# First layer's keys held twice with zeros for the other head, and the scores as five whole-array products

## The chip, the cores and the metric

The kernel runs on one core of one Trainium2 chip. The metric is the device time of one execution in microseconds (us). TensorE (PE in the rows; PEld is its weight load) multiplies into PSUM, VectorE is DVE, ScalarE is ACT, GpSimd is POOL, SyncE is SP and issues most DMAs.

## What is computed

The reference is a small early-fusion model over 8 images with their texts. What matters here, cut to its core:

```python
edge = abs_scharr(gray(x)); text = bigram_embed(x_txt)     # 256 + 128 tokens of width 256 per image
# layer 0: attention with 16 heads of 16 columns, then two MLPs (gelu; ternary relu)
q = q * cos + _rotate_half(q) * sin
k = k * cos + _rotate_half(k) * sin
scores = jnp.einsum('bhqd,bhkd->bhqk', q, k) / math.sqrt(hd)
scores = jnp.where(causal[None, None], -jnp.inf, scores)
attn = jax.nn.softmax(scores, axis=-1)
attn_out = jnp.einsum('bhqk,bhkd->bhqd', attn, v)
# layer 1: grouped attention with 16 heads of 64 columns and ALiBi, then a mixture of 8 experts
```

A sequence has S = 384 tokens, in NT = 3 tiles of P = 128. The scores are causal: query tile t needs keys of tiles 0 to t, so 128, 256 and 384 columns.

## The kernel before

**Stages.** A prologue loads the inputs, makes the grey images, the text rows and the first image's queries and keys. Then come 16 units of attention, written out by hand as one order of calls per engine: eight of layer 0 (`U_FIRST`, five times `U_MID0`, `U_SIX`, `U_SEVEN`) and eight of layer 1. A unit of layer 0 does the attention of image u, and in its gaps the MLPs of image u-1 (`s2`), the queries and keys of image u+1 (`s1`) and the convolution of image u+2 (`conv`). `U_FIRST` has no MLPs, `U_SIX` no convolution and with it no residual additions on GpSimd (L3212, L3216), `U_SEVEN` makes no keys of layer 0. The expert stage follows the last unit.

**Precision in layer 0.** Each head's 16 columns are split into an upper part and a rest. `stack_upper_half` (ACT, L1677) and `stack_lower_half` (DVE, L2314) write four combinations, 64 rows per head, into `stk_q` and `stk_k`. `stack_turned` (PE, L1042) turns them with four 128-column products per tile into a PSUM bank, which holds 4 pairs of heads. ScalarE copies the queries to `q0T` (L1692), VectorE the keys to `k0T` (L2327). Both have 128 partitions: rows 0 to 63 are the first head of a pair, 64 to 127 the second. The copies of a unit are named (hh, t): hh is the half of the heads, t the tile of tokens. Three copies of hh = 0 must be done before the unit's `scores_ahead`, or in the prologue before the first scores.

**Banks.** PSUM banks 0 to 2 hold the scores of a pair, 3 and 4 the turned probabilities, 5 the outputs. All dense products of the units (projections, MLPs, stacks) take banks 6 and 7 in turn: the planner `dense_units` lists them in PE's order, the k-th has bank 6 + k % 2. `wait_free` makes PE wait until the engine that copies a bank out has increased `freed`. A copy out that takes longer holds up PE's next use of that bank.

**Scores.** `pair_scores` (L950) gives the scores of heads 2p and 2p+1 with six products: stationary are 128 columns of the queries of one head (64 rows), moving are the keys of the same head. The order alternates the halves of the array. (s, 1) of both heads share bank 2; the semaphore `first_half` makes PE wait before it writes bank 2 for the second time. `filled[1]` is given after the fourth product, `filled[2]` after the fifth, `filled[0]` after the sixth. On VectorE `mask_max_of` (L2270) waits for `filled[s]` and `filled[2]`, adds the mask and finds the row maxima; ScalarE makes the exponentials, PE turns them (L978), ScalarE and VectorE copy them to `probsT` (L1733, L2429), and PE multiplies them with the values (L1013).

**Neighbours of the copies on VectorE's list in a unit of layer 0:** (0,0), take_turned(7), mask_max(10); mask_max(11), (0,1), take_turned(8), weigh(0); mask_max(12), (0,2), mask_max(13), stack_lower(1); mask_max(15), (1,0), hidden(0), hidden(1); take_turned(14), (1,1), mask_ahead(1); take_turned(15), (1,2), invert_last of the next unit.

**GpSimd in the prologue:** it clears `gray` (L3120) and `vpad` (L3121, 1536 elements a partition), then waits for the text index; later it gathers text rows and experts' rows with indirect DMAs. VectorE waits for `cleared` before the grey image (L2810).

Of the kernel before, what the change touches and what calls it, by code (L numbers as in the profile page):

```python
# [20 lines left out]
F32 = mybir.dt.float32  # L21
F32R = mybir.dt.float32r
# [5 lines left out]
P = 128  # L28
B = 8
# [4 lines left out]
S = IMG + TXT  # L34
NT = S // P
# [265 lines left out]
PAIRS = HEADS // 2  # L301
# [8 lines left out]
def at(u, per, k):  # L310


    reg, off = u
    return off * per + k if reg is None else reg * per + (off * per + k)


def moved(u, d):
    return u[0], u[1] + d
# [5 lines left out]
def early_fusion_kernel(nc, a, const, out):  # L324
# [10 lines left out]
    def sb(name, shape, dt=F32):  # L335
        at = offsets["top"]
        offsets["top"] = at + (width(shape) + 31) // 32 * 32
        return place(name, shape, dt, at)
# [9 lines left out]
    with ctx:  # L348
# [98 lines left out]
        rinvT = sb("rinvT", [P, S])  # L447
        qk_start = offsets["top"]
        q0T = sb("q0T", [P, 8, S], F32R)
        k0T = sb("k0T", [P, 8, S], F32R)  # L450
        (alibi,), _ = region(qk_start, ("alibi", [P, H1, S], F32))


# [59 lines left out]
        ps = [ctx.enter_context(nc.psum_tensor(f"bank{k}", [P, 512], F32)) for k in range(8)]  # L513


        filled = [sem(f"bank{k}_filled") for k in range(8)]
# [5 lines left out]
        cleared = sem("cleared")  # L522
# [42 lines left out]
        first_half = sem("first_half")  # L565
# [42 lines left out]
        def scores_place(n, t):  # L608

            if t == 1:  # L610
                return ps[2][:, 2 * P * (n % 2):2 * P * (n % 2) + 2 * P]
            return ps[n % 2][:, (3 * P, 0, 0)[t]:(4 * P, 0, 3 * P)[t]]
# [289 lines left out]
        def _(pe):  # L902
            mm, tr = nc.tensor.matmul, nc.tensor.transpose
# [46 lines left out]
            def pair_scores(layer, p, u):  # L950

                half = [slice(64 * s, 64 * s + 64) for s in range(2)]
                for b in range(3):
                    pe.wait_ge(freed[b], at(u, PAIRS, take0[b] + p))
                for s, t in ((0, 1), (1, 2), (0, 2), (1, 0), (1, 1), (0, 0)):
                    if layer == 0:
                        q, k = q0T[half[s], p, :], k0T[half[s], p, :]
                    else:
                        q, k = q1T[half[s], p, :], k1T[half[s], p // 4, :]
                    if (s, t) == (1, 1):  # L960
                        pe.wait_ge(first_half, at(u, PAIRS, p + 1))
                    last = mm(scores_place(s, t), q[:, P * t:P * (t + 1)], k[:, 0:P * (t + 1)], start=True, stop=True)  # L962
                    if (s, t) == (0, 1):
                        last.then_inc(first_half, 1)
                    if (s, t) == (1, 0):
                        last.then_inc(filled[1], 1)
                    if (s, t) == (1, 1):
                        last.then_inc(filled[2], 1)
                last.then_inc(filled[0], 1)
# [471 lines left out]
            for c in range(DC):  # L1441
                last = tr(ps[1][0:EMB, P * c:P * (c + 1)], proj_raw[:, c, :], ident)
# [5 lines left out]
            k = banks.bank(SETUP, "txt_index")  # L1448
# [3 lines left out]
            k = banks.bank(SETUP, "gamma")  # L1452
# [87 lines left out]
            bank = banks.bank(ROUTE, "thresholds")  # L1540
# [3 lines left out]
            for name, left in (("totals", "ones"), ("earlier", "before")):  # L1544
                bank = banks.bank(ROUTE, name)
                banks.wait_free(pe, ROUTE, name)
                mm(ps[bank][:, 0:2 * E * TILES], const_cols(left), sel_eq[:].rearrange("p k n -> p (k n)"),
                   start=True, stop=True).then_inc(filled[bank], 1)
# [3 lines left out]
            bank = banks.bank(ROUTE, "first_index")  # L1552
            banks.wait_free(pe, ROUTE, "first_index")
            for n in range(TILES):
                if n % 8 == 0:
                    pe.wait_ge(first_hot, n // 8 + 1)
                last = mm(ps[bank][0:CP, 0:CT], first_row[:, n, :], first_col[:, n, :],
                          start=(n == 0), stop=(n == TILES - 1))
# [492 lines left out]
        def _(dve):  # L2051
            v = nc.vector
# [193 lines left out]
            def first_norm_of(img_no, t):  # L2246
                normalise(LN_FIRST, img_no, mv_a, rstd_a, x1, h_in, t)
                then()
                moments(LN_ATTN0, stats_a, mv_a, x1, t)
# [76 lines left out]

            def take_stack_of(sec, i, hh, t):  # L2327
                k, f_ = bank_of(sec, f"stk{hh}_{t}_k", i)
                v.tensor_copy(k0T[:, 4 * hh:4 * hh + 4, P * t:P * (t + 1)],
                              k[:].rearrange("p (q n) -> p q n", q=4)).then_inc(f_, 1)  # L2330

            def values_of(sec, i, layer, t):
                k, f_ = bank_of(sec, f"v{layer}_{t}", i)
# [484 lines left out]
            k, f_ = bank_of(SETUP, "txt_index")  # L2818
# [27 lines left out]
            stack_lower_half(one, 0)  # L2846
            first_norm_of(two, 0)
            first_norm_of(two, 1)
            for t in range(NT):
                take_stack_of(PRO, 0, 0, t)  # L2850
            stack_lower_half(one, 1)
# [47 lines left out]
            k, f_ = bank_of(ROUTE, "by_group")  # L2899
            v.tensor_copy(by_group[:, 0:P], k[:, 0:P])  # L2900
            for h in range(2):
                rows, spot = slice(P // 2 * h, P // 2 * (h + 1)), slice(P + P // 2 * h, P + P // 2 * (h + 1))
                last = v.tensor_copy(by_group[rows, P:3 * P // 2], k[rows, spot])
# [3 lines left out]
            for r in range(SEARCH):  # L2907
                for q in range(STEPS):
                    last = ts(at_least[:, q, :], by_group[:], as_gate[:, q:q + 1], 0.0, ALU.is_ge, ALU.add,  # L2909
                              accum_out=cnt[:, q:q + 1])  # L2910
# [28 lines left out]
            k, f_ = bank_of(ROUTE, "thresholds")  # L2939
# [9 lines left out]
            k, f_ = bank_of(ROUTE, "totals")  # L2949
# [7 lines left out]
            k, f_ = bank_of(ROUTE, "earlier")  # L2957
# [50 lines left out]
            k, f_ = bank_of(ROUTE, "first_index")  # L3008
# [106 lines left out]
        def _(pool):  # L3115
            g = nc.gpsimd
# [2 lines left out]
                g.nop().then_inc(freed[bank], 1)  # L3119
            g.memset(gray[:], 0.0)  # L3120
            g.memset(vpad[:], 0.0).then_inc(cleared, 1)  # L3121

            banks.wait_taken(pool, SETUP, "txt_index")
            def gather_text(b):
# [260 lines left out]
```

## Time and profile before

| what | value |
|---|---|
| median of three runs | 1880.91 us (1877.96 to 1881.28) |
| the profiled execution | 1881.84 us, its span 1880.0 us |
| TensorE, matmul busy | 1751.2 us (93%) in 11231 |
| TensorE, weight load busy | 1427.0 us (76%) |
| VectorE busy | 1248.4 us (66%) in 4073 |
| ScalarE busy | 967.2 us (51%) |
| GpSimd busy | 545.7 us (29%) |
| mean granted clock of TensorE | 0.969 |
| indirect DMAs of GpSimd | 8 for the text, 3 x 64 for the experts |

Busy times of TensorE are modelled at their ends and overlap one another; two neighbouring starts say more than a duration. In a timeline a row that stands for several instructions has the start of the first and the time to the end of the last. Idle time in square brackets is that before the row, with what ended it.

### The profile page before, as it was taken

Reading aid. Unit: us, or ns where it says so; the run is one execution under the profiler, and the core shown is the slowest. Engines: PE = TensorE matmul, PEld = TensorE weight load, DVE = VectorE, ACT = ScalarE, POOL = GpSimd, SP = SyncE. Lnnn points to the kernel's source line nnn. Section 1 sums busy time; section 2 is a strip of 40 time slices with the busy share of each in tenths; the row PEclk is TensorE's granted clock in tenths of the full one; section 3 lists DMA queues with packets and bytes.
Section 4 is the critical chain, followed back from the end, with each engine's and each line's share of the span. In section 5 each row is a group of like instructions: output and inputs, shape, how many; then the busy total and the mean of one; then the engine's idle time right before and its main releaser. Section 6 shows DMA issues by size and latency. Waiting matters only on the chain.

```text
span 1880.0 us, 33649 instructions
## 1 busy us (share of the span) xinstructions
PE 1751.2 (93%) x11231; PEld 1427.0 (76%) x11231; DVE 1248.4 (66%) x4073; ACT 967.2 (51%) x2669; POOL 545.7 (29%) x763
## 2 busy tenths in 40 slices
PE   5788999999999999899999999993999999999997
PEld 3455677776867677688888888872898999899896
DVE  5678787777778775857767777667744555454542
ACT  1355657575756766656667666640234334333421
POOL 2352433424242410111111111010434434533431
PEclk9698999999999999999999999995999999999998
DMA  6111020101001010103001110012232321122210
GB/s 212 41 37 66 1 63 10 54 10 54 29 18 60 1 35 1 35 5 92 23 13 35 35 35 27 1 45 68 88 102 68 107 91 54 46 81 67 65 41 22
DMA packets 74244, 91.03 MB, mean 48 GB/s; under 512 B 16524, under 2 KB 64311, under 8 KB 74073
## 3 DMA queue, kind: packets, MB, share of 16 engines
q1 hardware_dynamic: 61464, 67.90, 11.1%
q0 software_dynamic: 9472, 16.77, 3.2%
q10 hardware_dynamic: 3136, 4.21, 0.6%
q8 instruction: 91, 1.49, 0.3%
q14 instruction: 81, 0.66, 0.1%
HBM read 71.02 MB, written 25.00 MB: 51 GB/s over the span
## 4 chain that ended last, share of the span: by engine, by line
PE 75%; issue 9%; DVE 7%; POOL 3%; ACT 2%; DVEq 2%; POOLq 1%; DMA 1%; SPq 0%; ACTq 0%
PE bank L1601 17%; PE bank L1030 16%; PE bank L1616 10%; PE bank L978 7%; PE bank L962 6%; PE bank L1013 6%; PE bank L1190 3%; PE bank L934 2%; PE bank L1052 2%; PE bank L989 1%; PE bank L914 1%; PE bank L935 1%; DVE at_least L2909 1%; POOL rstd_b L3136 1%; PE bank L1582 1%
## 5 line engine op out<-in xcount | busy, mean ns | idle before, releaser
L1725 ACT ACTIVATE probs<-probs,nmax 128x128 f32<-128x128 f32 (+2 forms) x768 | 381.5, 501 | 55.7 <-DVE nmax L2286 55.4
L978 PE MATMUL bank<-cst,probs 128*128 128x128 f32 x1536 | 235.1, 278 | 14.5 <-ACT probsT L1733 11.3
L978 PEld LDWEIGHTS bank<-cst,probs 128*128 128x128 f32 x1536 | 179.8, 142 | 48.1 <-issue 20.1
L3178 POOL COPY rinv<-rowsum 128x384 f32<-128x384 f32 x80 | 40.9, 511 | 563.6 <-DVE rowsum L2302 321.4
L1601 PE MATMUL bank<-xeT,gate_w 128*128 128x480 f32 x768 | 187.5, 379 | 0.5 <-issue 0.5
L1601 PE MATMUL bank<-xeT,up_w 128*128 128x480 f32 x768 | 186.8, 378 | 0.0
L3072 DVE TENSOR_TENSOR prod<-bank,sil 128x480 f32<-128x480 f32 x128 | 84.0, 657 | 147.6 <-PE bank L1601 146.8
L1616 PE MATMUL bank<-down_w,hT 128*120 128x256 f32 x1536 | 181.3, 280 | 0.0
L1616 PEld LDWEIGHTS bank<-down_w,hT 128*120 128x120 f32 x1536 | 179.9, 181 | 0.1
L1733 ACT COPY probsT<-bank 128x384 f32<-128x384 f32 x256 | 121.6, 475 | 107.4 <-PE bank L978 71.9
L1646 ACT ACTIVATE sil<-bank 128x480 f32<-128x480 f32 x128 | 73.0, 570 | 175.8 <-PE bank L1601 175.7
L2429 DVE COPY probsT<-bank 128x384 f32<-128x384 f32 x256 | 141.5, 553 | 30.3 <-PE bank L978 28.6
L1601 PEld LDWEIGHTS bank<-xeT,up_w 128*128 128x128 f32 x768 | 144.8, 189 | 21.6 <-DVE up_w L3004 0.2
L1601 PEld LDWEIGHTS bank<-xeT,gate_w 128*128 128x128 f32 x768 | 144.2, 189 | 21.5 <-issue 0.6
L1725 ACT ACTIVATION_READ_ACCUMULATOR probs<-probs,nmax 128x1 f32 x768 | 146.6, 191 | 0.0
L2286 DVE CUSTOM_DVE_ANT_0 probs<-bank,alibi 128x128 f32<-128x128 f32 (+2 forms) x384 | 141.7, 420 | 2.0 <-issue 0.3
L3354 POOL DMA_INDIRECT out<-ye,slot_token x64 | 75.5, 1180 | 229.7 <-DVE ye L3085 217.8
L2286 DVE CUSTOM_DVE_ANT_0 probs<-bank,cst 128x128 f32<-128x128 f32 (+2 forms) x384 | 140.9, 419 | 0.0
L962 PE MATMUL bank<-k1T,q1T 64*128 64x256 f32 (+2 forms) x768 | 100.5, 394 | 2.9 <-DVE nmax L2286 2.9
L3324 POOL DMA_INDIRECT xe<-xn_rows,slot_token x64 | 70.9, 1108 | 93.0 <-DVEq L3010 52.4
L962 PEld LDWEIGHTS bank<-k1T,q1T 64*128 64x128 f32 x768 | 83.3, 186 | 18.4 <-issue 12.9
L1013 PE MATMUL bank<-probsT,v 128*64 128x384 f32 (+2 forms) x768 | 97.0, 388 | 0.0
(350 smaller groups left out, 3422.3 us busy)
## 6 DMA issues: line engine op xcount, KB each, us to landing
gate_raw<-in_L_ffn_gate_w SPq DMA_DIRECT2D x8, 1024.0 KB, 4.8
up_raw<-in_L_ffn_up_w SPq DMA_DIRECT2D x8, 1024.0 KB, 6.9
down_raw<-in_L_ffn_down_w SPq DMA_DIRECT2D x8, 1024.0 KB, 5.7
img<-in_x SPq DMA_DIRECT2D x8, 768.0 KB, 5.1
residual_rows<-x SPq DMA_DIRECT2D x8, 384.0 KB, 2.5
residual_rows<-h_in SPq DMA_DIRECT2D x8, 384.0 KB, 3.6
xr<-residual_rows SPq DMA_DIRECT2D x8, 384.0 KB, 4.7
hr<-residual_rows SPq DMA_DIRECT2D x8, 384.0 KB, 3.6
```

The costliest lines, as they stand in the source:

```text
L962: last = mm(scores_place(s, t), q[:, P * t:P * (t + 1)], k[:, 0:P * (t + 1)], start=True, stop=True)
L978: last = tr(ps[bank][:, P * q:P * (q + 1)], probs[:, n % 4, SEG[t] + P * j:SEG[t] + P * (j + 1)], ident)
L1013: last = mm(ps[5][rows_o, P * j:S], w, probsT[:, n % 4, cols_j], start=first, stop=final)
L1030: last = mm(ps[bank][:, 0:width], x, w, start=(k == 0), stop=(k == len(pieces) - 1))
L1601: last = mm(ps[bank][:, 0:HALF], w[:, wp, c, P * m:P * (m + 1)], xeT[:, xp, c, HALF * hf:HALF * (hf + 1)], start=(c == 0 and k == 0), stop ...
L1616: last = mm(ps[bank][:, D * (j % 2):D * (j % 2) + D][0:CP], hT[:, j // 4, hp, m, CP * (j % 4):CP * (j % 4 + 1)], down_w[:, wp, m, :], star ...
L1725: last = f(p, p, ACT.Exp, bias=nmax[:, n % 4, t:t + 1], scale=-1.0, accum_out=rowsum[:, where, t:t + 1])
L1733: nc.scalar.copy(probsT[:, n % 4, 0:3 * P], ps[3][:, 0:3 * P]).then_inc(freed[3], 1)
L2286: last = v.tensor_tensor_reduce(out=probs[:, n % 4, seg(t)], in0=scores_place(n, t), in1=bias[:, P * (2 - t):S], scale=1.0, scalar=BIG, op ...
L2429: v.tensor_copy(probsT[:, n % 4, 3 * P:6 * P], ps[4][:, 0:3 * P]).then_inc(freed[4], 1)
L3072: tt(prod[:, q % 2, :], k[:, 0:HALF], sil[:, q % 2, :], ALU.mult).then_inc(f_, 1)
L3354: g.indirect_dma_start(out_rows, slots(e, j), ye[0:CP, j, :], None, bounds_check=T - 1, oob_is_err=False).then_inc(scattered, 16)
```

## The change

`k0T` gets a further dimension of two: for each head of the pair a whole 128-row key array, in which the 64 rows of the other head are zero. GpSimd clears all of it once, 128 partitions of 8 x 2 x 384 = 6144 elements. VectorE's copy of a key stack becomes two, each of 64 partitions, into the place of its head; the bank is given free behind the second. `pair_scores` in layer 0 multiplies all 128 rows of the queries (both heads) with such a key array; the zeros take the other head out. The middle tile does both heads at once, with 2 x 256 moving columns into all of bank 2. The order is: 512 columns, then per head 384 and 128; `filled[2]` comes after the first product, `filled[0]` after the third and `filled[1]` after the fifth. `first_half` is no more used in layer 0. SBUF for k0T grows by 12 KiB a partition; the scratch of GpSimd's descriptors is set to 4096 bytes.

```diff
-        k0T = sb("k0T", [P, 8, S], F32R)
+        k0T = sb("k0T", [P, 8, 2, S], F32R)
...
                 for b in range(3):
                     pe.wait_ge(freed[b], at(u, PAIRS, take0[b] + p))
+                if layer == 0:
+                    queries = [q0T[:, p, P * t:P * (t + 1)] for t in range(NT)]
+                    mm(ps[2][:], queries[1], k0T[:, p, :, 0:2 * P], start=True, stop=True).then_inc(filled[2], 1)
+                    for s, bank in ((0, 0), (1, 1)):
+                        mm(scores_place(s, 2), queries[2], k0T[:, p, s, :], start=True, stop=True)
+                        mm(scores_place(s, 0), queries[0], k0T[:, p, s, 0:P], start=True, stop=True).then_inc(filled[bank], 1)
+                    return
                 for s, t in ((0, 1), (1, 2), (0, 2), (1, 0), (1, 1), (0, 0)):
-                    if layer == 0:
-                        q, k = q0T[half[s], p, :], k0T[half[s], p, :]
-                    else:
-                        q, k = q1T[half[s], p, :], k1T[half[s], p // 4, :]
+                    q, k = q1T[half[s], p, :], k1T[half[s], p // 4, :]
                     if (s, t) == (1, 1):
-                        pe.wait_ge(first_half, at(u, PAIRS, p + 1))
+                        pe.wait_ge(first_half, at(moved(u, -B), PAIRS, p + 1))
...
                 k, f_ = bank_of(sec, f"stk{hh}_{t}_k", i)
-                v.tensor_copy(k0T[:, 4 * hh:4 * hh + 4, P * t:P * (t + 1)],
-                              k[:].rearrange("p (q n) -> p q n", q=4)).then_inc(f_, 1)
+                for s in range(2):
+                    rows_s = slice(64 * s, 64 * s + 64)
+                    last = v.tensor_copy(k0T[rows_s, 4 * hh:4 * hh + 4, s, P * t:P * (t + 1)],
+                                         k[rows_s, :].rearrange("p (q n) -> p q n", q=4))
+                last.then_inc(f_, 1)
...
             first_norm_of(two, 1)
+            dve.wait_ge(cleared, 2)
             for t in range(NT):
                 take_stack_of(PRO, 0, 0, t)
...
             g.memset(vpad[:], 0.0).then_inc(cleared, 1)
+            g.memset(k0T[:].bitcast(F32), 0.0).then_inc(cleared, 1)
...
-    nc = bacc.Bacc("TRN2", target_bir_lowering=False, num_devices=1)
+    nc = bacc.Bacc("TRN2", target_bir_lowering=False, num_devices=1, dynamic_dma_scratch_size=4096)
```

## Rows read from the trace of the kernel before

**Rows 1.** Busy time by stretch: span, PE, PEld, DVE, ACT, POOL, granted clock, DMA

```profile
359.20:445.30 86.10, 84.03 (x541) 63.05 (x541) 67.26 (x226) 54.98 (x160) 31.13 (x52) 1.00 0.11 35
...
137.00:157.00 20.00, 11.24 (x89) 8.56 (x89) 18.30 (x74) 14.91 (x52) 2.61 (x7) 0.80 0.00 1
```

**Rows 2.** Waits of PE in one steady unit: total us, times, longest

```profile
PE bank L1030 <- ACT relu L1646: 0.9, 1, 0.9
```

**Rows 3.** Timeline of PE: start us, us, what, count

```profile
421.72 0.66 PE L1052 MATMUL bank<-ident_r,stk_k 128*128 128x128 f32 x4
422.22 0.51 PE L978 MATMUL bank<-cst,probs 128*128 128x128 f32 x3
422.49 4.08 PE L1190 MATMUL bank<-f2T,hid_parts 128*128 128x256 f32 x32
426.40 0.56 PE L1052 MATMUL bank<-ident_r,stk_q 128*128 128x128 f32 x4
...
427.08 0.66 PE L1052 MATMUL bank<-ident_r,stk_k 128*128 128x128 f32 x4
427.67 0.82 PE L962 MATMUL bank<-k0T,q0T 64*128 64x256 f32 x6
428.43 0.53 PE L1013 MATMUL bank<-probsT,vpad 128*32 128x384 f32 x4
...
1500.37 1.44 PE L1601 MATMUL bank<-xeT,up_w 128*128 128x480 f32 x6
1501.65 1.44 PE L1601 MATMUL bank<-xeT,gate_w 128*128 128x480 f32 x6
```

**Rows 4.** The key copy, by its line: ns min/median/max, first and last start

```profile
L2329 DVE CAST k0T<-bank x48: 657/685/692, 80.0 to 679.7; 128x512 fp32r<-128x512 f32 x48
```

**Rows 5.** Groups of DVE by line and shape: busy us, mean ns

```profile
L2108 DVE TENSOR_TENSOR hashf<-hashf 8x128 f32<-8x128 f32 x1 | 0.3, 280 | 0.1
...
L2341 DVE TENSOR_TENSOR vpad<-bank,rows 128x128 f32<-128x128 f32 x6 | 1.4, 277 | 0.3 <-PE bank L1030 0.3
```

**Rows 6.** Timeline around copy (0,1) of a steady unit

```profile
392.66 0.69 DVE L2329 CAST k0T<-bank 128x512 fp32r<-128x512 f32 x1
...
393.28 0.56 DVE L2429 COPY probsT<-bank 128x384 f32<-128x384 f32 x1
...
393.57 0.61 PE L1052 MATMUL bank<-ident_r,stk_k 128*128 128x128 f32 x4
```

**Rows 7.** Timeline around copy (0,0)

```profile
385.79 0.69 DVE L2329 CAST k0T<-bank 128x512 fp32r<-128x512 f32 x1 [1.86 <-PE bank L1052]
...
386.66 0.86 PE L1030 MATMUL bank<-w,hidT 128*128 128x256 f32 x3
```

**Rows 8.** Timeline around copies (1,0) and (1,1)

```profile
410.53 0.69 DVE L2329 CAST k0T<-bank 128x512 fp32r<-128x512 f32 x1 [0.28 <-PE bank L1052]
...
411.35 0.94 PE L1030 MATMUL bank<-x_parts,f1T 128*128 128x384 f32 x4
...
411.58 2.15 POOL L3216 TENSOR_TENSOR h_in<-h_in,rows 128x768 f32<-128x768 f32 x1
...
411.96 1.99 DVE L2547 CAST hid_parts<-relu 128x384 fp32r<-128x384 f32 x1
...
423.09 0.68 DVE L2329 CAST k0T<-bank 128x512 fp32r<-128x512 f32 x1
```

**Rows 9.** Timeline of the prologue's key copies

```profile
81.86 0.69 DVE L2329 CAST k0T<-bank 128x512 fp32r<-128x512 f32 x1 [1.21 <-PE bank L1052]
...
92.31 1.11 PE L1052 MATMUL bank<-ident_r,stk_k 128*128 128x128 f32 x4 [1.51 <-DVE k0T L2329]
```

**Rows 10.** Start of the kernel: timeline of POOL and DVE, and L2065 by its line

```profile
1.84 1.38 POOL L3121 MEMSET vpad<- 128x1536 f32 x1
...
6.36 0.43 DVE L2232 TENSOR_SCALAR gray<-img 128x512 f32<-128x512 f32 x1 [2.40 <-DMA img<-in_x]
...
L2065 DVE TENSOR_SCALAR by<-tok x4: 272/277/766, 2.6 to 3.7; 8x258 int32<-8x258 int32 x4
```

## The prediction

> **What bounds the kernel now.** I read the page first (its figures are in the table above): TensorE is busy for 93% of the span, more than any other engine, though a busy TensorE is not one at its peak. Then I cut the first layer's stretch into its periods. One image's unit takes 86.1 us, and TensorE is busy for 84.0 of them at the full granted clock, VectorE for 67.3 [rows 1]. The waits of such a unit say the same: TensorE's longest is 0.9 us, on a ReLU of ScalarE [rows 2]. So in the steady units TensorE sets the time, and work given to VectorE is free only where nothing of TensorE waits for it. In the prologue and the first unit it is otherwise: between 137 and 157 us VectorE is busy for 18.3 of 20 us and TensorE for 11.2 [rows 1]; VectorE's own chain sets the pace there. Last I read the timelines around the touched lines, to see which wait stands right behind each.
>
> My sum is made against the profiled execution, 1881.84 us with a span of 1880.0; it lies 0.9 us above the median of the three runs, 1880.91.
>
> **Removed and put in its place: the products.** There were 384 half-array products (8 images, 8 pairs, 6 each). One set of six lasts 0.76 us from its first start to the next instruction's, from 427.67 to 428.43 [rows 3]. Going into it costs too: four 128-column products that are followed by a set take 0.59 us, the same four followed by transposes 0.50 [rows 3], so 0.09. Together 0.85 us. The five new ones are whole-array products of the same fast type with 512, 384, 128, 384 and 128 columns. From rows of that type: 32 products of 256 columns take 3.91 us, 0.122 each, and six of 480 take 1.28, 0.213 each [rows 3]. That is 0.41 ns a column, so 0.227 for 512 and 0.173 for 384; 128 columns take 0.11 to 0.125 (0.50 for four) [rows 3]. Sum 0.227 + 2 x 0.173 + 2 x 0.11 = 0.79 us. Bounds: from below the bare columns, 1536 at 2.4 GHz, 0.64 us; from above the four 128-column products' 0.125 for each short one and as much again between unequal widths, 0.95. I take 0.79, the nearest rows. So six of a unit's eight sets gain 0.06. The other two have a narrow neighbour (the 3-row products before scores(3), the 32-column products behind scores(1)) and keep that cost, so they lose 0.03 to 0.04. A unit gains 0.3 us, or 0.2 if the short products are at 0.125; I take 0.2 in each of seven units, **-1.4 us** (bounds -12 and +7).
>
> The set's row bears on a rule of the Trainium skill: 0.76 us for 1536 columns is more than the bare columns at the full clock, so the halves bought little. "TensorEngine Tiling (Array Packing)", sections Key Properties and Theoretical Speedup, says that products in different halves of the array run in parallel, up to twice as fast. By that rule the old set would need half its columns' time, 0.32 us, and the change would add 0.47 to each of 64 sets, 30 us; the measured 0.76 decides against it. No run here shows whether another order of the halves would come nearer.
>
> **Added: a second copy per key stack.** Each of 48 copies (PSUM to k0T, 128x512, 0.685 us [rows 4]) becomes two of 64 partitions, and the bank is freed behind the second. VectorE's duration does not follow the partitions: a 128-element tensor op takes 280 ns on 8 partitions and 277 on 128 [rows 5]. So each half costs what the whole did. One behind another, such copies start 0.61 apart (392.66 copy, 393.28 next op [rows 6]); I take +0.60 us. From below, 0.30 would be half the copy at half the partitions, and 0 if the two overlapped wholly; from above 0.69. 48 x 0.60 is 29 us of VectorE. What of it lies on TensorE's path:
>
> (0,0) of a steady unit: the copy ends at 386.48 and the next product into the same bank starts at 386.66 [rows 7]; TensorE's weight load waits for that bank. With 0.60 more the bank comes free at 387.08, TensorE starts near 387.19: +0.53. (0,1): copy from 392.66 to 393.35, the next stack product into that bank at 393.57 [rows 6]: free at 393.95, start at 394.06: +0.49. (1,0): the copy ends at 411.22, the product starts at 411.35 [rows 8]: +0.55, but here something takes it back. TensorE later waits 0.9 us for a ReLU [rows 2] that waits for hid_parts; the cast before it takes 1.99 us because a GpSimd op runs until 413.73 [rows 8]. A cast that starts 0.6 later ends with that op all the same, and the later wait shrinks by what the earlier one grew. I take 0 (bound +0.55). (0,2), (1,1), (1,2): the next user of the bank comes 0.6 us later or more. The tightest is (1,1): its copy ends at 423.77 [rows 8], the bank's next product is the seventeenth of those that start at 422.49 [rows 3], so 424.45. I take 0 (bound 0.1 together). Behind each copy VectorE's queue holds a probsT copy or a mask_max, which TensorE and ScalarE need; VectorE's idle spots (19 us a unit) absorb those. So 1.02 a unit, five units: **+5.1 us**. The sixth unit has no residual additions on GpSimd (no convolution), so (1,0) counts as well: **+1.6**.
>
> Prologue: the six stack products of a half alternate two banks. The copy of 81.86 ends at 82.55 and would end at 83.15; the next key product, 0.05 us behind it, moves along. At 92.31 such a product starts after TensorE has sat idle for 1.51 us on the copy before it [rows 9]. Each copy but (0,2) hands its +0.60 on: 5 x 0.60, **+3.0 us**. First unit: copies (0,0), (0,1), (0,2) lie in VectorE's closed stretch, +1.8; (1,0) half hidden, +0.3; (1,1) before mask_ahead, for which scores(1) waits, +0.6: **+2.7 us**.
>
> **Added: a memset of 6144 elements a partition on GpSimd.** vpad's 1536 take 1.38 us [rows 10], so four times as many 5.2 to 5.5 us, from 3.2 to about 8.5 us. GpSimd's own next work is at 34 us, and VectorE's wait for `cleared` comes at about 80 us: both hidden. But VectorE isn't: an op that ran beside the vpad memset took 766 ns against 277 for its like [rows 10]. The grey-image ops start at 6.36 [rows 10], at the head of the chain that ends last (grey image, halo transfer, convolution). The next token op, at 3.28, would stand until 8.5 and push the grey image to about 9: +2.6; if the token ops slip through first, +1.8. I take **+2.2** (bounds 0 and 2.8; a gain is excluded, as it only adds work).
>
> **Moved and dropped waits.** The wait on `first_half` goes with the old sets, priced within them; the second layer's keeps its meaning with counts shifted by one layer. Head 0's scores are ready after three products of five, some 0.25 us sooner; VectorE's mask_max is not what steady TensorE waits for, so 0. The descriptor scratch for GpSimd's indirect transfers shrinks; nothing in the trace shows it in use: 0, with a rival below.
>
> Sum: -1.4 + 5.1 + 1.6 + 3.0 + 2.7 + 2.2 = **+13.2 us**, 1894.1 against the median (1895.0 against the profile).
>
> **Rivals.** A change of 0.2% (3.8 us) is about what a measurement of this kernel can tell from none.
> (1) The bank waits stay but the new set runs at its columns' pace, 0.64: 48 sets x 0.21 and 16 x 0.11 save 12 instead of 1.4: +2.6 to +4 us, about 1884 to 1885, at the edge of no change. For: TensorE is the bound. Against: no row of that type is under 0.12 us for 256 columns.
> (2) The half copies cost half each, so nothing is added: -1.4 + 2.2 = +0.8, 1881.7, no change. Against: the 8-partition row.
> (3) Faster: the new set saves more than the copies cost. Place: the sets in the steady units, at 0.64 us (-12). It decides by over 3.8 us only if a copy adds under (12 - 3.8 - 2.2) / 20.7 = 0.29 us (my copy terms are 20.7 times 0.60). With copies at 0.15 it gives 12.4 / 4 - 12 + 2.2 = -6.7, 1874.
> (4) More stalls: (1,0) isn't absorbed in the five middle units (+2.8), or the longer idle of the first unit keeps TensorE's clock low for longer (the granted clock was 0.80 of full speed there on average [rows 1]): +3 to +6, 1897 to 1900.
> (5) The smaller scratch makes GpSimd wait in the expert stage, where indirect transfers follow one another: some us on each of eight experts, beyond 1900.
>
> **How the numbers follow.** Forecast 0.60; rival (1) 0.13, (2) 0.08, (3) 0.05, (4) 0.11, (5) 0.03. Slower: 0.60 + 0.11 + 0.03 + 0.10 of (1) = 0.84; same: 0.08 + 0.03 = 0.11; faster 0.05. The range reaches from rival (1) to rival (4), 1884 to 1900; it leaves out (2), (3) and (5), 0.16 in all.
>
> **What would show it.** Products: 320 in place of 384 on the new lines, a set at 0.79 us start to start. Copies: 96 of 64x512 at 0.69 us. Waits: TensorE on k0T near (0,0) and (0,1) of each unit, 0.5 us each; a unit's period 86.1 grown to 86.9. The grey image ending at 10 to 11 in place of 8.3 us. The start of the steady part 7 to 8 us later. I am wrong if the unit's period doesn't grow, or if a half copy takes under 0.5 us.

## The result, and the profile after

The changed kernel takes 1890.22 us (median of six runs, 1887.33 to 1891.88) where the kernel before, run beside it, takes 1881.10: ratio 1.0049, 95% interval 1.0037 to 1.0061, so +9.2 us (+7.0 to +11.5). Timed a second time it gave 1.0059 (1.0043 to 1.0075). It is slower, as forecast, and the time lies in the range; 1894.1 was 4 us too much. That closeness is in part luck, errors of opposite sign, as the runs show: the copies cost 6 to 9 us more than the forecast had, a gain of 5.6 us at the very end of the program stood in it at 0, and the products saved 2.7 us more.

| what | before | after |
|---|---|---|
| the profiled execution's span | 1880.0 us | 1886.4 us |
| TensorE, matmul busy | 1751.2 us in 11231 | 1750.0 us in 11167 |
| TensorE, weight load busy | 1427.0 us | 1444.2 us |
| VectorE busy | 1248.4 us in 4073 | 1283.2 us in 4121 |
| mean granted clock | 0.969 | 0.966 |
| a middle unit of layer 0 | 86.1 us | 87.25 us |
| GpSimd's last instruction, a DRAIN (from the trace's records) | 7.90 us | 2.34 us |

The middle unit that answers to [rows 1], cut at the same instruction (columns as there):

```profile
366.68:453.93 87.25, 84.53 (x533) 65.47 (x533) 70.09 (x232) 55.29 (x160) 30.85 (x52) 1.00 0.11 34
```

The unit is 1.15 us longer at the same full clock. TensorE is busy for 0.5 us more with 8 products fewer, VectorE for 2.8 us more with six copies more. TensorE's waits in it, beside [rows 2]:

```profile
PE bank L1034 <- DVE k0T L2335: 0.9, 2, 0.5
PE bank L914 <- DVE xh_b L2212: 0.7, 1, 0.7
PE bank L1056 <- DVE k0T L2335: 0.4, 1, 0.4
PE bank L982 <- ACT probsT L1737: 0.3, 1, 0.3
PE bank L1034 <- ACT relu L1650: 0.2, 1, 0.2
```

Three new waits for the copies of the key stacks, 1.3 us together, and the wait for the ReLU fallen from 0.9 to 0.2. The forecast had two of the three stalls, and the absorption of the third. The places, in time order, TensorE's rows and VectorE's copies:

```profile
394.57 0.45 PE L1034 MATMUL bank<-w,hidT 128*128 128x256 f32 x1 [0.50 <-DVE k0T L2335]
...
402.04 0.55 PE L1056 MATMUL bank<-ident_r,stk_k 128*128 128x128 f32 x3 [0.37 <-DVE k0T L2335]
...
420.37 0.98 PE L1034 MATMUL bank<-x_parts,f1T 128*128 128x384 f32 x4 [0.40 <-DVE k0T L2335]
...
422.88 1.87 PE L1034 MATMUL bank<-x_parts,f1T 128*128 128x384 f32 x8 [0.16 <-ACT relu L1650]
```

```profile
393.03 1.39 DVE L2335 CAST k0T<-bank 64x512 fp32r<-64x512 f32 x2 [1.72 <-PE bank L1056]
...
400.60 1.39 DVE L2335 CAST k0T<-bank 64x512 fp32r<-64x512 f32 x2
...
418.93 1.39 DVE L2335 CAST k0T<-bank 64x512 fp32r<-64x512 f32 x2 [0.29 <-PE bank L1056]
```

A pair of half copies takes 1.39 us where the whole one took 0.69 [rows 4]. Over all 96:

```profile
L2335 DVE CAST k0T<-bank x96: 650/689/695, 77.3 to 693.4; 64x512 fp32r<-64x512 f32 x96
```

(shortest, median and longest ns): 64 partitions cost what 128 did. The operation behind the copy starts 0.60 to 0.67 us after a whole copy's start, and 1.41 to 1.45 after a pair's, so VectorE's order moves back by 0.8 us each time. The set of products that answers to the one at 427.67 [rows 3]:

```profile
436.11 0.45 PE L957 MATMUL bank<-k0T,q0T 128*128 128x512 f32 x1
436.40 0.34 PE L959 MATMUL bank<-k0T,q0T 128*128 128x384 f32 x1
436.57 0.23 PE L960 MATMUL bank<-k0T,q0T 128*128 128x128 f32 x1
436.63 0.39 PE L959 MATMUL bank<-k0T,q0T 128*128 128x384 f32 x1
436.87 0.22 PE L960 MATMUL bank<-k0T,q0T 128*128 128x128 f32 x1
437.02 0.53 PE L1017 MATMUL bank<-probsT,vpad 128*32 128x384 f32 x4
```

From its first start to the next instruction's it lasts 0.91 us, not 0.79; the old one lasted 0.76. The unit's eight new sets last 0.75, 0.90, 0.84, 0.86, 0.84, 1.05, 0.84 and 0.84 us (means of four middle units), the old ones 0.75 or 0.76 each. What they gain lies ahead of them (the run of the products alone, below).

The start of the program, VectorE and then GpSimd:

```profile
2.68 6.44 DVE L2069 TENSOR_SCALAR by<-tok 8x258 int32<-8x258 int32 x4 [1.23 <-DMA tok<-in_x_txt]
9.05 0.41 DVE L2236 TENSOR_SCALAR gray<-img 128x512 f32<-128x512 f32 x1
```

```profile
3.15 5.22 POOL L3130 MEMSET k0T<- 128x6144 f32 x1
```

Four token operations that take 1.3 us without the memset last 6.44, and the grey image begins at 9.05 in place of 6.36 [rows 10].

The end of the program: the last indirect store of the kernel before is issued at 1869.11 and the span ends at 1880.0, 10.9 us later; after the change,

```profile
1880.95 1.01 POOL L3363 DMA_INDIRECT out<-ye,slot_token  x1 [0.30 <-issue]
```

and the span ends at 1886.4, 5.4 us later. From 1384 us on all of TensorE's starts and this store are 11.8 us later than before, the end of the span only 6.4. Between the two lies GpSimd's last DRAIN, 7.90 us long before and 2.34 after; it begins 2.8 us behind the last store's start in both.

**Two profiled executions carry different pieces of low clock**, so a difference of starts is read stretch by stretch. From the start of one unit's scores to the next one's, the five stretches of middle units and the sixth run at full clock, and repeat from execution to execution of one kernel to 0.1 us, the sixth to 0.3. The first 165 us and the end of layer 0 do not repeat. Nor does the stretch from 1260 to 1384 us: over it the changed kernel's profile gains 1.9 us on that of before, by shorter pieces of low clock. The profile has no record of the clock before its first piece of full clock (49.9 us in the kernel before) and counts that time as full, though products there run at the pace of the low clock; so its mean granted clock is a little too high.

### The profile page after: what moved, and what is told of

It reads as the page before. It is cut to its first block, busy times and chain, and to the rows that moved or that the text cites. A ratio compares the mean times of both kernels' runs of the same rounds, so it can differ in the third digit from the quotient of the medians.

```text
span 1886.4 us, 33571 instructions
## 1 busy us (share of the span) xinstructions
PE 1750.0 (93%) x11167; PEld 1444.2 (77%) x11167; DVE 1283.2 (68%) x4121; ACT 969.8 (51%) x2669; POOL 549.3 (29%) x764
## 3 DMA queue, kind: packets, MB, share of 16 engines
q1 hardware_dynamic: 61464, 67.90, 11.1%
## 4 chain that ended last, share of the span: by engine, by line
PE 75%; issue 9%; DVE 8%; POOL 2%; DVEq 2%; ACT 2%; POOLq 1%; DMA 0%; SPq 0%; ACTq 0%
PE bank L1605 17%; PE bank L1034 16%; PE bank L1620 10%; PE bank L982 7%; PE bank L1017 6%; PE bank L966 5%; PE bank L1194 3%; PE bank L934 2%; PE bank L993 1%; PE bank L1056 1%; PE bank L914 1%; DVE k0T L2335 1%; PE bank L959 1%; PE bank L935 1%; DVE at_least L2917 1%
## 5 line engine op out<-in xcount | busy, mean ns | idle before, releaser
L3333 POOL DMA_INDIRECT xe<-xn_rows,slot_token x64 | 71.6, 1118 | 89.6 <-DVEq L3018 51.8
```

## The experiments

Each was timed in five rounds beside the kernel before. The ratio is the one on record, with its 95% interval; it is not the quotient of the two medians (for e2_copies that would be 22.5 us and not 21). A difference in us below is the ratio's unless medians are named. "Middle unit" is the distance of two units' starts at full clock, from the trace.

| kernel | median us | before, beside it | ratio (95%) | middle unit | last DRAIN |
|---|---|---|---|---|---|
| e1_scratch | 1875.68 | 1879.38 | 0.9976 (0.9964 to 0.9988) | 86.06 | 2.34 |
| e2_copies | 1901.92 | 1879.38 | 1.0112 (1.0095 to 1.0130) | 87.78 | 7.90 |
| e3_products | 1875.89 | 1879.38 | 0.9978 (0.9966 to 0.9990) | 85.62 | 7.90 |
| e4_memset | 1878.92 | 1879.38 | 0.9998 (0.9987 to 1.0008) | 86.07 | 2.34 |
| e5_clear_act | 1892.22 | 1879.80 | 1.0061 (1.0048 to 1.0074) | 87.27 | 2.34 |
| e6_two_engines | 1884.74 | 1879.80 | 1.0023 (1.0013 to 1.0032) | 86.73 | 2.34 |
| e7_scratch2k | 1874.03 | 1879.80 | 0.9963 (0.9952 to 0.9975) | 86.06 | 0.71 |
| e8_behind | 1880.86 | 1879.80 | 1.0002 (0.9992 to 1.0013) | 86.53 | 2.34 |
| e9_change_again | 1892.65 | 1880.29 | 1.0059 (1.0043 to 1.0075) | 87.25 | 2.34 |
| e10_clear_again | 1890.30 | 1880.29 | 1.0049 (1.0035 to 1.0063) | 87.28 | 2.34 |

### The scratch alone

```diff
-    nc = bacc.Bacc("TRN2", target_bir_lowering=False, num_devices=1)
+    nc = bacc.Bacc("TRN2", target_bir_lowering=False, num_devices=1, dynamic_dma_scratch_size=4096)
```

> The kernel before with the descriptor scratch of 4096 bytes and nothing else. Theory A: the scratch sets how long GpSimd's last instruction, a DRAIN behind the last indirect store, takes (7.90 us before, 2.34 us after the change), so the time falls by 5.5 us, a ratio near 0.997, and all starts up to the last indirect store stay within 0.5 us apart from pieces of low clock. Rival B, my forecast: 0 us, the drain stays at 7.9 us (its length then hangs on what the queue still has to do). Rival C: waits of GpSimd in the expert stage, over +5 us.

The DRAIN took 2.34 us and the time fell by 4.5 us (2.3 to 6.8). The distance from the last store to the end of the span:

```profile
span 1877.8 us, 33649 instructions
```

```profile
1872.40 1.01 POOL L3354 DMA_INDIRECT out<-ye,slot_token  x1 [0.31 <-issue]
```

so 5.4 us, as after the change, in place of 10.9. Theory A holds: the last instruction's length follows the size of the scratch, the work in the queue being the same. Whether more or less work would change it too, no run tells. The expert stage was not longer: from 1384 us on, all starts of TensorE in the changed kernel stand 11.84 to 11.86 us behind those of before, to the last expert's end; in this run 3.28 to 3.30.

### A still smaller scratch

```diff
+    nc = bacc.Bacc("TRN2", target_bir_lowering=False, num_devices=1, dynamic_dma_scratch_size=2048)
```

> The kernel before with a descriptor scratch of 2048 bytes. Theory A: GpSimd's last DRAIN grows with the scratch's size (16384 bytes 7.90 us if that is the size before, 4096 bytes 2.34 us, a slope of 0.45 ns a byte), so it takes 1.4 us here and the time is 6.5 us under the kernel before. Rival B: the drain stays near 2.3 us. Rival C: the smaller scratch makes indirect transfers wait for room in the expert stage, an expert's 61 us grow, and the time is above that of the kernel before.

The DRAIN took 0.71 us, shorter than the straight line's 1.4 (from 4096 to 2048 bytes it lost 0.80 ns a byte; the expectation's 0.45 above that takes the size before as 16384, which no run prints), and the time fell by 7.0 us (4.7 to 9.0). The expert stage did not grow: from 1384 us on all starts of TensorE stand 0.43 us ahead of those of before. This kernel has the lowest median of all that were run, and of the change it has only the last line, with another size.

```profile
span 1872.7 us, 33649 instructions
```

```profile
1868.97 1.01 POOL L3354 DMA_INDIRECT out<-ye,slot_token  x1 [0.30 <-issue]
```

### The copies alone

```diff
-                v.tensor_copy(k0T[:, 4 * hh:4 * hh + 4, P * t:P * (t + 1)],
-                              k[:].rearrange("p (q n) -> p q n", q=4)).then_inc(f_, 1)
+                for s in range(2):
+                    rows_s = slice(64 * s, 64 * s + 64)
+                    last = v.tensor_copy(k0T[rows_s, 4 * hh:4 * hh + 4, P * t:P * (t + 1)],
+                                         k[rows_s, :].rearrange("p (q n) -> p q n", q=4))
+                last.then_inc(f_, 1)
```

> The kernel before with each copy of a key stack cut into two of 64 partitions, the old six products, no zeros, the old scratch. Theory A: the copies alone make the longer first layer: a middle unit +1.0 to +1.2 us, the prologue +3.0, the first unit +2.7 to +3.7, the sixth +1.6 to +2.2, in all +12.4 to +14.5 us, 1893.5 to 1895.5. Rival B: a part of the growth of a unit comes from the new products, so that a middle unit grows by 0.6 us or less here and the time by under 9 us. The GpSimd drain at the end stays at 7.9 us if the scratch sets it.

The time rose by 21 us (17.9 to 24.4), more than the whole change costs, and a middle unit by 1.71:

```profile
371.94:459.72 87.78, 85.06 (x541) 63.28 (x541) 71.15 (x232) 55.30 (x160) 30.77 (x52) 1.00 0.11 34
```

The copies alone make the loss; theory A holds for its place and was low for its size (1.0 to 1.2 us a unit and 12.4 to 14.5 in all expected). The starts of TensorE's products in this unit against those of before show where: +0.66 at the product behind copy (0,0), +0.56 behind (0,1), +0.68 behind (1,0) and +0.43 at a ReLU's bank soon after, of which 0.91 comes back at 415.25 (time of before), +0.16 at the MLP's second product behind (1,1), and +0.25 less 0.11 near 433. Sum 1.72. The last of these stands at a product (`wo,o0T`) for which the waits name no key copy; that it comes from VectorE's lateness behind (1,2), and not from a bank, is likely and not shown. From unit to unit the stretches of this run are longer than those of before by 3.6 us (prologue), about 3.1 (first unit, with the clock in it), 2.45, four times 1.71 and 2.3: 18 of the 21 us. The rest lies within the interval and was not traced.

### The products alone

```diff
+                if layer == 0:
+                    twice = k0T[:, p, 0:2 * P].unsqueeze(1).broadcast_to([P, 2, 2 * P])
+                    mm(ps[2][:], queries[1], twice, start=True, stop=True).then_inc(filled[2], 1)
+                    for s, bank in ((0, 0), (1, 1)):
+                        mm(scores_place(s, 2), queries[2], k0T[:, p, :], start=True, stop=True)
+                        mm(scores_place(s, 0), queries[0], k0T[:, p, 0:P], start=True, stop=True).then_inc(filled[bank], 1)
+                    return
```

> The five whole-array products in place of the six half-array ones, with the old key array and one copy per stack; left out are the zeros, so each head's scores are the sum of both heads' scores. Theory A: a set at 0.79 us where it was 0.76 plus 0.09 at its entry, -1.4 us in all (-0.2 a middle unit). Rival B: the set runs at its columns' pace, 0.64 us, and a middle unit is 1.5 us shorter, -12 us in all. Rival C: the new set costs 0.95 us, a middle unit +0.8, +7 us in all.

The time fell by 4.1 us (1.9 to 6.4), a middle unit by 0.45:

```profile
356.31:441.93 85.62, 83.45 (x534) 65.31 (x533) 66.09 (x226) 54.96 (x160) 31.11 (x52) 1.00 0.11 35
```

None of the three had it: the sign is A's, the size between A and B. The set that gains most, scores(5) behind `xTb,w`, in the kernel before and here:

```profile
377.65 1.78 PE L1030 MATMUL bank<-xTb,w 128*128 128x384 f32 x5
379.36 0.82 PE L962 MATMUL bank<-k0T,q0T 64*128 64x256 f32 x6
380.11 0.59 PE L1030 MATMUL bank<-xTb,w 128*128 128x384 f32 x1
```

```profile
376.24 0.69 PE L958 MATMUL bank<-k0T,q0T 128*128 128x512 f32 x1
...
377.28 0.54 PE L1035 MATMUL bank<-xTb,w 128*128 128x384 f32 x1
```

The old set lasts 0.75 us, the new one 1.04, and yet TensorE comes out of it 0.15 us ahead, because it goes in 0.45 sooner relative to the work ahead. The sets that gain nothing are the two with a narrow neighbour. Scores(3), behind the products of 3 rows, in the kernel before and here:

```profile
447.12 0.69 PE L935 MATMUL bank<-halo_gray,edge_w 3*128 3x256 f32 x2
447.74 0.83 PE L962 MATMUL bank<-k0T,q0T 64*128 64x256 f32 x6
448.50 1.55 PE L1030 MATMUL bank<-wqkv,xTa 128*128 128x512 f32 x3
```

```profile
444.04 0.69 PE L935 MATMUL bank<-halo_gray,edge_w 3*128 3x256 f32 x2
444.67 0.50 PE L958 MATMUL bank<-k0T,q0T 128*128 128x512 f32 x1
...
445.52 1.07 PE L1035 MATMUL bank<-wqkv,xTa 128*128 128x512 f32 x2
```

From the first row to the last it was 1.38 us and is 1.48. Now take each set from the start of the last product ahead of it to the start of the first behind it (means of four middle units). The eight sets, scores(0) to scores(7), took 1.02, 0.96, 0.95, 1.06, 0.95, 1.17, 0.95 and 0.96 us, and take 0.93, 1.01, 0.86, 1.16, 0.87, 1.07, 0.86 and 0.86: six gain 0.08 to 0.10, scores(1) and scores(3) lose 0.05 and 0.10, together 0.40 of the unit's 0.45. In six of the eight sets the product ahead starts 0.03 to 0.17 us before the new set, where it was 0.20 to 0.42; ahead of scores(1) 0.11 for 0.21, and ahead of scores(3) 0.30 in both. So the cost of the half-array set lay ahead of its first start more than in it, and the four-against-four comparison of [rows 3] (0.09) had only a part of it.

### Copies whole, and further work of VectorE behind them

```diff
                 v.tensor_copy(k0T[:, 4 * hh:4 * hh + 4, P * t:P * (t + 1)],
                               k[:].rearrange("p (q n) -> p q n", q=4)).then_inc(f_, 1)
+                v.tensor_copy(spare[0:64, t], cst[0:64, 0:704])
```

> The kernel before with the small scratch; each copy of a key stack is whole and frees the bank as before, and behind it VectorE makes a further copy of like length from constants in SBUF (64 x 704, about 0.7 us) that nobody reads. Theory A: the bank's hold makes the stalls, not VectorE's time: a middle unit grows by 0 to 0.5 us in place of 1.7, and the time, with the scratch's -5, is between -5 and +3 us. Rival B: VectorE's lost time makes them: a middle unit grows by 1.2 us or more, the time by +10 us or more.

The added copy took 0.51 us, not 0.7, but for (1,0), where it ran beside a GpSimd operation and took 0.87. A middle unit grew by 0.46 in place of 1.71, the time by 0.4 us (-1.5 to +2.4), with the small scratch in it. No bank is held longer, but VectorE's added work is not as much as in e2_copies: 2.3 us a unit against 3.9 (69.5 and 71.2 us busy, 67.3 before). The next operation starts some 0.4 us later than before at five of the six places, where e2_copies has 0.8; only behind (1,0) it is 0.8 in both. All of the 0.46 arises there, in TensorE's wait for a ReLU:

```profile
PE bank L1031 <- ACT relu L1647: 1.2, 1, 1.2
```

against 0.9 [rows 2]. Theory A holds: at (0,0) and (0,1) TensorE no longer stops, and there the traces of the change name the key copy as what it waited for. Most of a unit's 1.71 us is the time for which a bank is held. The exact split, 1.25 against 0.46, is not shown: VectorE's loss was only half as large here at five places, and behind (1,0) the added copy was itself longer, beside a GpSimd operation.

### The second head's copy on ScalarE

```diff
+            def take_second_keys_of(sec, i, hh, t):
+                name = f"stk{hh}_{t}_k"
+                banks.wait_filled(act, sec, name, i)
+                bank = banks.bank(sec, name)
+                nc.scalar.copy(k0T[64:P, 4 * hh:4 * hh + 4, 1, P * t:P * (t + 1)],
+                               ps[bank][64:P, :].rearrange("p (q n) -> p q n", q=4)).then_inc(freed[bank], 1)
...
-        eng.wait_ge(self.freed[bank], i * per + (base + n + 1))
+        eng.wait_ge(self.freed[bank], i * per + (base + n + uses(name)))
```

> As the one before, but the copies of the second head's keys (partitions 64 to 127) are made by ScalarE beside VectorE's of the first head's, and the bank is free when both are through. Theory A: what costs the time is how long a bank is held, not VectorE's time: the stalls go, a middle unit is 0.2 to 0.5 us shorter than before the change (the products' gain), and the time is 8 to 10 us under the kernel before (products -4, scratch -5), near 1871. Rival B: ScalarE becomes late instead (its exponentials and ReLUs each begin some 0.5 us later six times in a unit), a middle unit stays above 86.5 us and the time is near or above that of before.

```profile
PE bank L986 <- ACT probsT L1748: 0.6, 1, 0.6
PE bank L918 <- DVE xh_b L2238: 0.5, 1, 0.5
PE bank L1038 <- ACT relu L1654: 0.5, 1, 0.5
PE bank L1038 <- ACT rinvT L1652: 0.3, 1, 0.3
PE bank L997 <- ACT q0T L1711: 0.2, 1, 0.2
```

Rival B, in the main. The waits for `k0T` are gone from this list (one weight load still waits 0.3 us for ScalarE's copy), the middle unit is 86.73, and in their place stand waits for ScalarE, whose order got a copy of 0.58 us (64x512; 48 of them) at six places. Against e5_clear_act, which differs from it in this alone, the time is 7 us lower (1.0061 to 1.0023). It remains 1.1 us a unit above the products alone, and above the kernel before: of it 0.56 us arise at a wait for `rinvT` and 0.38 at one for `q0T`, both of which ScalarE writes. Other places in ScalarE's order were not tried.

### The memset: alone, replaced, and repeated

Alone, with the large array and the small scratch (e4_memset); with ScalarE's zeros in its place in the changed kernel (e5_clear_act and e10_clear_again, the same kernel):

```diff
-            g.memset(k0T[:].bitcast(F32), 0.0).then_inc(cleared, 1)
...
+            act.wait_ge(cleared, 1)
+            zero = vpad[:, 0, 0:1, 0:1].to_broadcast([P, 8, S])
+            nc.scalar.copy(k0T[0:64, :, 1, :], zero[0:64])
             for hf in range(2):
                 edges(SETUP, 0, (None, 0), hf)
+            nc.scalar.copy(k0T[64:P, :, 0, :], zero[64:P]).then_inc(cleared, 1)
```

> The large key array with its memset and VectorE's wait for it, and the small scratch that makes room for it; old products in half of that array, one copy per stack. Theory A: the grey image is 2.7 us late and so is the convolution, and the clock in the prologue decides how much of it is left: between 0 and +2.7 us up to the last indirect store; with the drain's -5.5 the time is -5.5 to -2.8 us. Rival B: the later start shifts a rise of the granted clock to before 36 us, and the first layer begins earlier than in the kernel before, up to -3 us at 80 us.

> The changed kernel with the zeros written by ScalarE (two copies of 64 partitions x 3072, in its idle stretches at 21 to 35 us) and no memset on GpSimd. Theory A: the grey image is back at 6.4 us, the first layer begins some 3 us earlier at equal clock, and the time is about 3 us under the changed kernel's (1886 to 1888, +5.5 to +7.5 us against the kernel before); the middle units keep their +1.17 us. Rival B: the memset's delay was given back by the clock, and the time stays at +9 us. Together with the runs of the single parts this also shows whether they add up: copies +21, products -4, scratch -4.5 give +12.5 us (rival C).

> The changed kernel once more, beside the next one on the same chip, since the memset's cost came out with both signs (+3.2 us between the two kernels with the small scratch, -2.3 us between the change and the version with ScalarE's zeros, which were timed on different occasions). Theory A: the memset costs 2 to 3 us whatever else is changed, so this kernel is 2 to 3 us above the next. Rival B: the clock gives its delay back in the full change, and the two agree within 1 us. Rival C: the earlier result holds, and this one is 2 us or more below the next.

> The version with ScalarE's zeros once more. Theory A: 2 to 3 us under the changed kernel. Rival B: within 1 us of it. Rival C: 2 us or more above it. In each case the middle units stay at 87.24 us, and any difference lies before the second unit, where the granted clock changes.

In the trace the delay at the start is plain. Without the memset (e5_clear_act) the same four operations take

```profile
2.63 1.33 DVE L2073 TENSOR_SCALAR by<-tok 8x258 int32<-8x258 int32 x4 [1.18 <-DMA tok<-in_x_txt]
6.37 0.43 DVE L2240 TENSOR_SCALAR gray<-img 128x512 f32<-128x512 f32 x1 [2.41 <-DMA img<-in_x]
```

and the grey image is back at 6.37. How much of this delay is left is seen where the clock changes at the same places. The profiles of e4_memset and of the kernel before are such a pair (the scratch differs between them too), all pieces of low clock up to 166 us being 2.8 to 2.9 us later with the memset. The longest of them, before and in e4_memset:

```profile
70.40:101.10 30.70, 20.86 (x79) 17.14 (x79) 17.74 (x63) 14.05 (x43) 7.66 (x13) 0.50 0.12 39
```

```profile
73.30:104.00 30.70, 20.85 (x79) 17.11 (x78) 17.83 (x63) 14.03 (x43) 7.66 (x13) 0.50 0.12 39
```

The first scores begin at 84.55 us in the one and at 87.51 in the other, 2.96 later: at equal clock the delay of 2.6 us at the grey image reaches the first scores whole. In the time it is less plain. The two comparisons made side by side give +3.2 us (e4_memset's median against e1_scratch's, by their ratios 4.1) and +2.4 (e9_change_again against e10_clear_again, by their ratios 1.9, with intervals that overlap). The third, -2.0 (1890.22 against e5_clear_act's 1892.22), is between two occasions. So theory A of the last two, 2 to 3 us, has the better evidence, but with this scatter rival B, nothing, isn't excluded. The time expected of e4_memset, -5.5 to -2.8 us, was missed: it came out at -0.4 (-2.4 to +1.5), as the scratch gave 4.5 us and not 5.5, and the memset took more than the 2.7 of its upper bound. The time expected of e5_clear_act, +5.5 to +7.5, was missed too, at +11.5; its middle units kept their 1.2 us.

One profile of one kernel says little of its prologue. The first scores begin at 84.03 and 89.53 us in two profiles of the changed kernel, at 84.31 and 87.24 in two with ScalarE's zeros, at 88.24 in e2_copies, and in the kernels with whole copies and no memset at 84.55 (before) and 81.1 to 82.8 (four others). The clock differs between them: in the changed kernel's first profile it is full from 23.6 to 33.9 us (six products of the convolution take 1.56 us), in the kernel before it was still low then (six such take 2.93). That is not the memset's doing: the first piece of full clock begins at 23.6, 35.0 and 52.8 us in the three profiles with it, and anywhere from 20.4 to 51.1 in the nine without it.

The parts add up, as far as their intervals tell: +21 (copies), -4.1 (products), -4.5 (scratch) make +12.5, against +11.5 (9.0 to 13.9) for e5_clear_act, which has these three and no memset (rival C of its expectation), and +9.2 (6.6 to 11.8) for the same kernel as e10_clear_again.

## Why the prediction was right and where it was not

**The range and the sign** came from the copies' hold on banks, and that mechanism is what the runs show: the copies alone cost 21 us, and the three largest stalls stand at the places that were named, two of them forecast as stalls and one, (1,0), as absorbed.

**Products** (forecast -0.2 a unit, -1.4 in all): -0.45 a unit, -4.1 in all. The term was mis-sized twice over. The step "0.227 + 2 x 0.173 + 2 x 0.11 = 0.79" failed; the eight sets last 0.75 to 1.05, 0.86 on average. And the entry was worth more than the 0.09 of [rows 3]: up to 0.42 us lay between the product ahead and a half-array set, and 0.03 to 0.17 is left in six of eight. That the two sets with a narrow neighbour lose was right ("so they lose 0.03 to 0.04"; measured 0.05 and 0.10).

**Half copies** (forecast +0.60 each): +0.70, as the pair's 1.39 us shows. That a half costs as much as the whole was right. The 0.61 between starts in [rows 6] was the copy's distance to an operation of another kind; two copies of this kind stand 0.70 apart, and the operation behind them comes 0.8 later.

**Steady units** (forecast +1.02 of copies): +1.71. (0,0) and (0,1) cost 0.66 and 0.56 for 0.53 and 0.49. The 0 for (1,0) was nearly right, 0.20 net: the wait behind it did shrink from 0.9 to 0.2, but a second one of 0.43 came between. The 0 for (1,1) and (1,2), "bound 0.1 together", failed: 0.16 and 0.14. What was not costed is that VectorE's own time matters behind (1,0); e8_behind shows 0.46 there with no bank held longer.

**Sixth unit** (forecast +1.6 less the products' 0.2): +2.2. **Prologue** (+3.0): +3.6, of which 2.17 lie ahead of scores(0) and 1.43 between scores(0) and scores(1); the latter distance is 11.6 us in every kernel with whole copies and 13.0 in every one with pairs. Five pairs at 0.70 are 3.5. **First unit** (+2.7): +2.9 between the two profiles, from its scores(1) to the next unit's first scores, with the clock's share in it: that stretch takes 68.2 to 73.0 us in six profiles with whole copies and 71.6 to 73.8 in five with pairs, so the term is not measured to better than 2 us.

**Memset** (+2.2): the grey image moved by 2.69 us, near the upper bound, and at equal clock the first scores by 2.96 (e4_memset); the times show 2.4 and 3.2 us side by side, and -2.0 between two occasions.

**Scratch** (0, "nothing in the trace shows it in use"): this step failed. It is the term that was put at nothing, and the runs show -5.6 us of DRAIN in its place, 4.5 us of time. The profile's groups and timeline do not show a DRAIN; but 10.9 us between the last store and the end of the span could be read off the trace of before, and the forecast left them unread. Rival (5) looked at the right object in the wrong stage and with the wrong sign.

Put together with what was measured: 3.6 (prologue) + 2.9 (first unit) + 2.0 (the first middle stretch, which is 81 us long before) + 4 x 1.2 (the next four) + 2.2 (sixth) - 0.5 (the products in the last unit) - 5.6 (drain) = +9.4 us, and 0 to 3 for the memset; measured +9.2 and, the second time, +11.1. The forecast's +13.2 had the copies 6 to 9 us too low (12.4, where e2_copies has 21 and this sum, with the products' 4.1 taken out, some 19), the products' gain 2.7 too small, and the drain missing.

**Rivals.** (1) and (3) fall, as the new sets ran at 0.75 to 1.05 us and not at their columns' pace of 0.64; (2) falls with the 689 ns of a half copy; (4) was right in kind, as there were more stalls, but (1,0) took 0.20 of the 0.55 a unit that it priced; (5) falls, as TensorE's starts in the expert stage kept their distances.

The rule of the Trainium skill that was weighed, "TensorEngine Tiling (Array Packing)", section Theoretical Speedup (products in the two halves up to twice as fast), was not borne out: replacing the halves' set by whole-array products gained time in e3_products, where by that rule it would have cost 30 us (the prediction's estimate). Only this one order of the halves was run, with a wait for the shared bank in it.

## What to carry to other kernels

A PSUM bank is given free behind the last part of its copy-out, and here a half copy takes as long as a whole one, so splitting the copy by partitions doubled the hold (1.39 us for 0.69). Price such a split by which product is waiting for that bank, and test it by putting added work behind the release, as long as the work it stands for (here it was shorter, and a unit grew by 0.46 us against 1.71). When work is moved to an engine at half load (ScalarE is busy for 51% here), look at what waits in its order, not at its share. And read what lies between the last useful instruction and the end of the span: a size given in the program's set-up took 5.6 to 7.2 us off there in the traces, and 4.5 to 7.0 off the time, as much as the new products (4.1) or more.

## What was not expected of the hardware

- GpSimd's last DRAIN takes 7.90 us with the descriptor scratch at the size it has when none is given, 2.34 with 4096 bytes and 0.71 with 2048, the queue's work being the same. It is the same to 0.01 us in all kernels with one size.
- A copy from PSUM of 64 partitions takes as long as one of 128: 689 ns on VectorE against 685; on ScalarE 581 ns for 64x512 against 587 for 128x512 (e6_two_engines).
- Beside a GpSimd memset of 5.22 us, four VectorE operations on 8 partitions took 6.44 us together, 1.33 without it; ScalarE wrote the half of these zeros that is needed in two copies of 2.73 and 2.75 us, and VectorE's operations of 8 partitions beside the first of them took 0.21 to 0.28 us, as they did without it.
- Two profiled executions of one and the same kernel had the first scores at 84.03 and 89.53 us, with TensorE's granted clock full from 23.6 us on in the one and from 35.0 on in the other, while their middle units agreed to 0.05 us.
